# Sliding attention with alternating heads, value products one clip later, and the copy of the late transposed probabilities moved behind all exponentials

## The reference

```python
def _sliding_window_attn(q, k, v):          # 32 clips, 8 heads, 125 positions, 16 features
    for o in range(-32, 33):
        s = einsum('bhsd,bhsd->bhs', q, roll(k, -o)) * scale
        s = where((pos + o >= 0) & (pos + o < S), s, -inf)
    ...
    p = softmax(scores, axis=-1)
    ...
    out = out + p[..., idx:idx+1] * roll(v, -o)
...
qkv  = layernorm(h) @ W_qkv + b_qkv
h    = h + attention(q, k, v) @ W_proj + b_proj
out  = h + layernorm(h)                      # the last stage, whose other columns lie beyond the 128 there are
```

## Time and profile before

| what | value |
|---|---|
| median of 3 runs | 547.76 us (547.48 to 548.02) |
| profiled run | 550.68 us |
| span of the profiled run | 548.9 us, mean granted clock 0.947 |
| busy: PE, PEld, DVE, ACT, POOL | 503.3, 355.3, 408.9, 358.4, 329.2 us |
| exponentials of the windows (L972) | first starts at 390.8, last at 535.3 us |

### The profile page before, as it was taken

How to read it: one execution, slowest core, us unless ns; L and a number is a source line. 1 busy time by engine, 2 the same in 40 slices (tenths; PEclk the granted TensorE clock), 3 DMA queues, 4 the chain that set the end, 5 groups by cost and what they waited for, 6 DMA issues and landing times.

```text
span 548.9 us, 13987 instructions
## 1 busy us (share of the span) xinstructions
PE 503.3 (92%) x4554; PEld 355.3 (65%) x4554; DVE 408.9 (74%) x1728; ACT 358.4 (65%) x1072; POOL 329.2 (60%) x367
## 2 busy tenths in 40 slices
PE   6998899999998599999999999997599999999983
PEld 4778666666665357766667776655367766776762
DVE  3797757888886367787877777865369988898993
ACT  5985558889887244454455445453578888888881
POOL 2860647778886556776666676663126555565654
PEclk9999559999999699999999999999779999999997
DMA  4440212222222010000000000000000000000000
GB/s 163 138 161 11 64 34 51 56 62 62 63 60 75 20 37 20 19 20 22 35 22 20 19 20 20 1 1 1 0 2 2 20 21 20 13 11 21 20 21 20
DMA packets 21946, 19.89 MB, mean 36 GB/s; under 512 B 14210, under 2 KB 18466, under 8 KB 21746
## 3 DMA queue, kind: packets, MB, share of 16 engines
q1 hardware_dynamic: 21298, 18.28, 11.6%
q10 hardware_dynamic: 576, 0.71, 0.4%
HBM read 16.81 MB, written 2.18 MB: 35 GB/s over the span
## 4 chain that ended last, share of the span: by engine, by line
PE 44%; DVE 15%; issue 4%; ACT 2%; POOL 2%; POOLq 0%; DVEq 0%; ACTq 0%
PE quad L802 10%; PE quad L779 9%; PE bank L824 6%; PE bank L888 4%; PE bank L899 4%; DVE quad L1156 4%; PE bank L905 3%; PE quad L771 2%; PE bank L880 2%; DVE z_all L1186 2%; DVE otok L1168 2%; DVE st_all L1188 2%; DVE wmax L1156 2%; PE bank L793 1%; PE bank L817 1%
## 5 line engine op out<-in xcount | busy, mean ns | idle before, releaser
L476 POOL TENSOR_SCALAR put<-keyb,c 100x1000 f32<-100x1000 bf16 x32 | 89.0, 2782 | 47.9 <-DMA keyb<-key_scratch 26.3
L972 ACT ACTIVATE wprobs<-quad,wmax 125x125 f32<-125x125 f32 x256 | 75.5, 372 | 19.7 <-DVE wmax L1156 19.7
L1156 DVE CUSTOM_DVE_ANT_0 quad<-quad,c 125x125 f32<-125x125 f32 x256 | 66.1, 311 | 9.1 <-PE quad L847 9.1
L609 ACT ACTIVATE probs<-quad,negmax 100x250 f32<-100x250 f32 x128 | 58.3, 467 | 21.8 <-DVE negmax L561 20.9
L779 PE MATMUL quad<-h1T,w 128*128 128x500 f32 x128 | 61.9, 609 | 0.7 <-ACT hid L943 0.6
L802 PE MATMUL quad<-w,hid 128*125 128x128 f32 x512 | 58.8, 273 | 0.1
L802 PEld LDWEIGHTS quad<-w,hid 128*125 128x125 f32 x512 | 57.3, 188 | 0.8 <-issue 0.5
L1058 POOL TENSOR_TENSOR kbd<-wkT,c 128x250 f32<-128x250 f32 x32 | 19.2, 600 | 53.0 <-ACT wkT L980 53.0
L491 PE MATMUL bank<-c,probs 100*125 100x100 f32 x256 | 48.3, 316 | 2.2 <-ACT probs L609 1.4
L491 PEld LDWEIGHTS bank<-c,probs 100*125 100x125 f32 x256 | 36.8, 209 | 20.6 <-issue 13.2
L943 ACT ACTIVATE hid<-quad,vec_cols 128x500 f32<-128x500 f32 x64 | 43.0, 675 | 7.4 <-PE quad L779 4.1
(11 more groups left out here) (131 smaller groups left out, 1267.9 us busy)
## 6 DMA issues: line engine op xcount, KB each, us to landing
keyb<-key_scratch SPq DMA_DIRECT2D x64, 97.7 KB
xa<-xT SPq DMA_DIRECT2D x8, 500.0 KB, 3.6
xt<-xtok SPq DMA_DIRECT2D x16, 250.0 KB
out<-o_all SPq DMA_DIRECT2D x7, 250.0 KB
w<-weights SPq DMA_DIRECT2D x1, 1024.0 KB, 7.2
vec_rows<-rows SPq DMA_DIRECT2D x1, 448.0 KB, 5.2
c<-consts ACTq DMA_DIRECT2D x1, 428.5 KB, 6.5
w<-weights ACTq DMA_DIRECT2D x1, 192.0 KB, 4.2
```

Of the source, the lines that this page charges most:

```text
L476: nc.gpsimd.tensor_scalar(put[u % 3][:, :, :], keyb[p][:, :, :], c[0:ROWS, CONST["sidx"]], None, ALU.is_equal).then_inc(put_done, 1)
L609: nc.scalar.activation(probs[p][:, ch, :], s_bank[ch][0:ROWS, 0:L], ACT.Exp, bias=negmax[p][:, ch:ch + 1], accum_out=rowsum[p][:, ch:ch + ...
L972: ins = nc.scalar.activation(probs[p][:, j, :], s_of(j), ACT.Exp, bias=negmax[p][:, j:j + 1], scale=-1.0)
L1156: ins = nc.vector.tensor_tensor_reduce(s_of(j), s_of(j), c[0:LH, CONST["band"]], 1.0, OFF, ALU.add, ALU.min, negmax[p][:, j:j + 1])
```

## The change

Heads are worked on in the order 0, 2, 4, 6, 1, 3, 5, 7 (`ORDER`), so that neighbours in time lie in different banks. The transposed probabilities and the products are stored in that order, and the scaling of `otok` puts the heads back. Each mask and each exponential signals by itself (the counts go by 8 in place of 4), and the mask of the fifth to eighth head waits for the exponential of the head four places before it. The value products work on clip u-2 in window u, and everything behind them is one window later too. There is a third buffer `vo`, `y_of` and the projection lie in other columns, and the drain is one window longer.

The order changes too. On TensorE the `y_a` transposes stand ahead of the late transposes, and the value products go between the key and query products and the value matmul, ahead of `y_of`:

```diff
+                if within(u, 3, B + 3):
+                    pe.wait_ge(oT_done, u - 2)
+                    for i in range(2):
+                        ins = nc.tensor.transpose(y_a[:, 128 * i:128 * i + 128], oT[:, LH * i:LH * i + LH], ident)
+                    ins.then_inc(otok_ready, 1)
...
+                if within(u, 2, B + 2):
+                    wait(pe, otok_done, u - 2)
+                    wait(pe, oT_done, u - 2)
+                    pe.wait_ge(pT0_done, u - 1)
+                    pe.wait_ge(pT1_done, u - 1)
+                    pe.wait_ge(v_done, u - 1)
...
+                    for j in range(H):
+                        ins = nc.tensor.matmul(y_bank[CW * (j % 4):CW * (j % 4) + CW, LH * (j // 4):LH * (j // 4) + LH],
+                                               vo[(u - 2) % 3][:, ORDER[j], :], probsT[p][:, j, :], start=True, stop=True)
+                    ins.then_inc(pv_ready, 1)
+
                 if within(u, -1, B - 1):
                     wait(pe, qT_done, min(u + 2, B))
                     wait(pe, v_done, u + 1)
                     nc.tensor.matmul(x_v, n3T_all[:, LH * (u + 1):LH * (u + 1) + LH], w[:, WEIGHT["wv"]], start=True, stop=True).then_inc(v_ready, 1)
 
-                if within(u, 2, B + 2):
-                    pe.wait_ge(otok_done, u - 1)
+                if within(u, 3, B + 3):
+                    pe.wait_ge(otok_done, u - 2)
                     nc.tensor.transpose(y_of, otok[:, :], ident[0:LH, 0:LH]).then_inc(oF_ready, 1)
```

On ACT `woT` moves from behind `vo` to behind `kT`, and the exponentials of all heads stand together ahead of the copy of the late transposed probabilities:

```diff
+                def exponents(lo, hi):
+
+                    for k in range(lo, hi):
+                        j = ORDER[k]
+                        act.wait_ge(min_done, H * u + k + 1)
+                        nc.scalar.activation(probs[p][:, j, :], s_of(j), ACT.Exp, bias=negmax[p][:, j:j + 1], scale=-1.0).then_inc(exp_done, 1)
...
                 if within(u, 0, B):
                     wait(act, pT0_ready, u - 1)
-                    exponents(0)
-                    exponents(1)
+                    exponents(0, 8)
                 if within(u, 1, B + 1):
                     act.wait_ge(pT1_ready, u)
                     wait(act, pv_ready, u - 2)
                     nc.scalar.activation(probsT[1 - p][:, 4:8, :].rearrange("p h l -> p (h l)"), t_bank[1][0:LH, 0:4 * LH], ACT.Copy).then_inc(pT1_done, 1)
-                if within(u, 0, B):
-                    exponents(2)
-                    exponents(3)
```

On DVE the masks come as 2, 4 and 2 with the reciprocal and `otok` behind the first two and `oF` behind the next four, and `z_all` goes ahead of the copy:

```diff
+                if within(u, 0, B):
+                    dve.wait_ge(scores, u + 1)
+                    mask_and_min(0, 2)
...
+                if within(u, 0, B):
+                    mask_and_min(2, 6)
+                if within(u, 3, B + 3):
+                    dve.wait_ge(oF_ready, b + 1)
+                    wait(dve, proj_ready, b)
                     nc.vector.tensor_scalar(oF[:, :], y_of, col("wv_b"), None, ALU.add).then_inc(oF_done, 1)
                 if within(u, 0, B):
-                    mask_and_max(3)
+                    mask_and_min(6, 8)
+                if within(u, 3, B + 3):
+                    dve.wait_ge(proj_ready, b + 1)
...
+                    nc.vector.tensor_tensor(z_all[:, b:b + 1, :], y_proj.unsqueeze(1), z_all[:, b:b + 1, :], ALU.add).then_inc(z_done, 1)
+                if within(u, 0, B):
                     dve.wait_ge(pT0_ready, u + 1)
                     wait(dve, pv_ready, u - 1)
                     nc.vector.tensor_copy(probsT[p][:, 0:4, :].rearrange("p h l -> p (h l)"), t_bank[0][0:LH, 0:4 * LH]).then_inc(pT0_done, 1)
```

More of the change, by code:

```diff
@@ L725, in ffn_and_window @@
         x_k, x_q, x_v = x_bank[:, 0:LH], x_bank[:, 128:128 + LH], x_bank[0:LH, 256:256 + D]
-        y_a, y_of, y_proj = y_bank[0:LH, 256:512], y_bank[:, 0:LH], y_bank[0:LH, 256:256 + D]
+        y_a, y_of, y_proj = y_bank[0:LH, 256:512], y_bank[:, 256:256 + LH], y_bank[0:LH, 384:384 + D]
+        ORDER = (0, 2, 4, 6, 1, 3, 5, 7)
         def s_of(head):
@@ L856, in window @@
                     for j in range(4):
-                        ins = nc.tensor.transpose(t_bank[1][0:LH, LH * j:LH * j + LH], probs[pm][:, 4 + j, :], ident[0:LH, 0:LH])
+                        ins = nc.tensor.transpose(t_bank[1][0:LH, LH * j:LH * j + LH], probs[pm][:, ORDER[4 + j], :], ident[0:LH, 0:LH])
                     ins.then_inc(pT1_ready, 1)
-                if within(u, 2, B + 2):
[L861 to L864, removed]
                 if within(u, -2, B - 2):
@@ L887, in window @@
                     for j in range(4):
-                        ins = nc.tensor.transpose(t_bank[0][0:LH, LH * j:LH * j + LH], probs[p][:, j, :], ident[0:LH, 0:LH])
+                        ins = nc.tensor.transpose(t_bank[0][0:LH, LH * j:LH * j + LH], probs[p][:, ORDER[j], :], ident[0:LH, 0:LH])
                     ins.then_inc(pT0_ready, 1)
[L891 to L904, removed]
+                if within(u, 3, B + 3):
+                    pe.wait_ge(oF_done, u - 2)
                     nc.tensor.matmul(y_proj, oF[:, :], w[:, WEIGHT["wp"]], start=True, stop=True).then_inc(proj_ready, 1)
             in_turn(pe, ffn, window)
-            for u in range(B, B + 2):
+            for u in range(B, B + 3):
                 at(window, u)
@@ L980, in window @@
                     nc.scalar.activation(kT[:, :], x_k, ACT.Identity, bias=col("wk_b")).then_inc(kT_done, 1)
+                if within(u, 3, B + 3):
+                    act.wait_ge(pv_ready, u - 2)
+                    wait(act, otok_ready, u - 3)
+                    wait(act, z_done, u - 3)
+                    nc.scalar.activation(oT[:, :], y_bank[:, 0:2 * LH], ACT.Copy).then_inc(oT_done, 1)
+                if within(u, -1, B - 1):
                     wait(act, scores, u)
@@ L984, in window @@
                     act.wait_ge(v_ready, u + 1)
[L985 to L991, removed]
+                    wait(act, pv_ready, u - 2)
+                    nc.scalar.activation(vo[u % 3][:, :, 0:HD], x_v.rearrange("p (h f) -> p h f", h=H), ACT.Copy).then_inc(v_done, 1)
                 if within(u, 0, B):
                     wait(act, pT0_ready, u - 1)
-                    exponents(0)
-                    exponents(1)
+                    exponents(0, 8)
                 if within(u, 1, B + 1):
@@ L1073, in _ @@
             in_turn(pool, ffn, window)
-            for u in range(B, B + 3):
+            for u in range(B, B + 4):
                 at(window, u)
@@ L1148, in window @@
                 u, _, _ = shift(h, p, 0)
[L1149 to L1157, removed]
-                if within(u, 0, B):
-                    mask_and_max(0)
-                    mask_and_max(1)
@@ new lines, in window @@
+                if within(u, 3, B + 3):
+                    dve.wait_ge(otok_ready, b + 1)
+                    nc.vector.reciprocal(rinv[:, :], y_a.rearrange("p (h f) -> p h f", h=H)[:, :, HD]).then_inc(rinv_done, 1)
+                    dve.wait_ge(rinv_done, b + 1)
+                    wait(dve, oF_ready, b)
+                    nc.vector.tensor_tensor(otok[:, :].rearrange("p (k c f) -> p c k f", k=4, c=2),
+                                            y_a.rearrange("p (c k f) -> p c k f", c=2, k=4)[:, :, :, 0:HD],
+                                            rinv[:, :].rearrange("p (c k) -> p c k", c=2).unsqueeze(3).to_broadcast([LH, 2, 4, HD]),
+                                            ALU.mult).then_inc(otok_done, 1)
```

69 lines of the change are left out of this document (30 added, 39 removed).

## The result

The changed kernel took 562.16 us (561.53 to 562.58, 4 runs) against 547.62 for the kernel before: 1.027 times as long, 95% interval 1.0247 to 1.0293. The forecast was 563.3.

What follows compares the result with a forecast made beforehand. TensorE's late `y_of` holds DVE's `oF` and the masks behind it: 1.41 + 2.22 + 0.32 + 0.89 = 4.84 us a window; 13.6 - 2.0 + 3.9 = +15.5 us on 547.76 gives 563.3 us, range 558.5 to 567 (73%).

Steps and rivals of the forecast that it cites:

- The chain: Last exponential, late copy, `kT`, `woT`, `y_a`, TensorE's work before `y_of`, `oF`, two masks, last exponential: window 4.84 us against 4.37.
- The cause: `y_of` comes late on TensorE, so DVE waits at `oF` with the last two heads' masks queued behind it.
- The idle time: DVE stands idle before `oF`, waiting for TensorE's `y_of`: 0.6 us a window.
- What the change saves does not reach the end of the window: First exponential starts 0.25 us sooner, but the last goes by the last mask; order and single signals costed at nothing.
- Number of windows and ends: 29 windows at +0.47 give +13.6 us, windows 1 and 2 save 2.0, the longer drain adds 3.9: +15.5 us.
- The circle through the projection: `oF`, projection, `z_all`, copy, statistics, next masks: not what is waited for, with 0.2 us to spare.
- Neighbours on DVE: Operations around `oF` overlap; under the skill page's drain rule they would not, some 0.2 us more, window 5.0 us.
- the clock: Expected to stay at 1.00 (2.4 GHz); rival that it falls to 1.2 GHz for good, +60 us, 2%.
- The rivals: `woT` not holding 8%, `oF` not waited for 5%, no change 3%, clock falls 2%, slower than forecast 9%.
- `oF` was waited for: Second rival denied this: `y_of` ends before DVE's sixth mask is done, window 4.0 us, time 539, 5%.
- The first rival: `woT` does not hold TensorE, `y_a` starts behind the scores: window 4.48 us, time 552.9, 8%.
- the hold: On TensorE `y_a` waits for `woT` until T + 1.41, though TensorE is free at T + 1.05.

Runs made afterwards that it cites:

- the run with `oF` late: Changed kernel with DVE's `oF` behind the last two heads' masks and the early transposes' copy ahead of `z_all` again: window 4.35 us, 551.0 us in all.
- the run with pairs: Changed kernel with heads in natural order and both exponentials of a bank waiting for both its masks: window 5.06 us, 571.16 us in all.
- the run with the copy in the middle: Changed kernel with the late copy back between the fourth and fifth exponential on ACT: window 4.53 us, 555.21 us in all.
- the kernel before with the copy last: Kernel before with only the late copy moved behind all exponentials, value products still of clip u-1 in window u: 624.04 us, ratio 1.1381.

## Why the prediction was right, point by point

**The chain.** It foretold four parts from one `exponential` start to the next: 1.41 to the start of `y_a`, 2.22 to `y_of`, 0.32 to `oF`, 0.89 to the last exponential. The rows after give 471.34 - 469.93 = 1.41, 2.19, 0.31 and 0.90. The sum was 4.84 and is 4.81. 469.93 is 474.74 less a window. The value products with the change of shape took 1.11 from 472.10 to 473.21 with keys and queries, foretold 1.14. Six runs each altered one link, and each moved the window by what the chain had made one expect of that link, to within 0.05 us, up (two) or down (four).

**The cause.** DVE's `oF` waits for `y_of`, with two masks behind it. In the run with `oF` late a window is 0.46 us shorter, all of the 0.44 that the change had added. The idle time was put at 0.6, and the profile has 0.44. That counts from the end of the sixth mask's read, 473.25 + 0.14 = 473.39. From the read's start, which is nearly where the prediction's sum has DVE ready, it is 0.59. The term enters no sum.

**What alternation is worth.** Here the prediction's words failed: "What the change saves does not reach the end of the window", with the single signals costed at nothing. Its own arithmetic had the saving in it, because it let the last exponential follow 0.04 us behind the last mask's read. With signals by pairs both exponentials of the bank wait for that mask, and the last starts 0.25 later, which is what the run with pairs gives back (5.06). Without that saving the sum would have come out at 5.1. A step that reads "costs nothing" should be checked for what the sum would be without it.

**Number of windows and ends.** Foretold 13.6 for 29 windows, -2.0 for the first two and +3.9 for the drain, 15.5 in all. By the rows it is 29 x 0.44 = 12.8 for the windows, 10.3 - 12.8 = -2.5 for the rest between first and last exponential, and +4.6 for the drain, together 14.9. The windows were put 0.8 too high and the drain 0.7 too low, and these two nearly cancelled. The -2.5 has two parts. From the first exponential of window 1 to that of window 3 it was 410.68 - 401.16 = 9.52 us and is 404.28 - 396.47 = 7.81, which is 1.7 of the 2.0 foretold. The prediction left out the other part: the last two windows before the drain are shorter than 4.81, with last exponentials at 532.47, 537.10 and 541.23, so 4.63 and 4.13.

**The circle through the projection** was put at 0.2 us to spare. The trace of the changed kernel bears it out. Before the change the reciprocal starts together with the read of the mask ahead of it, at 467.67; in the changed kernel that read starts at 471.65 and the reciprocal at 471.87, right behind the end of `y_a` at 471.34 + 0.48 = 471.82. So DVE had 0.22 us to spare there.

**Neighbours on DVE, and the clock.** `oF` starts at 473.84, takes 0.35, and the mask behind it starts at 474.10, before its end; the window is 4.81. The page "VectorE: DVE Perf Modes" of the Trainium skill, section "The DRAIN you can't avoid", says that the next operation does not start until the pipe is empty, and by that a window would have been 5.0 us, an estimate of the prediction. The same section also says that a next operation that is not held starts earlier, which the prediction didn't mention, and the trace agrees with this second sentence. The clock stayed at 1.00 from 450 to 500 us. The page "TensorE: Matmul & The Clock Gate" of the Trainium skill, section "Part 1: The HAM clock gate (the "warmup" mystery)", says that the throttled state is the default and activity releases it; nothing in this trace speaks against that. The prediction had TensorE's waits elsewhere: it named 0.36 us before `y_a` and about 0.4 before the projection, and the trace has 0.21 before `y_a`, none before the projection and 0.52 before the scores.

**The rivals.** None came. `woT` did hold TensorE (0.21 us in each window), the clock held, and `oF` was waited for. The first rival's window of 4.48, without `woT`'s hold, is close to what the run with the copy in the middle reached, 4.53. That puts the hold at 0.28 us, where the prediction had 1.41 - 1.05 = 0.36: its scores start 0.42 behind the last exponential's start, and they start at 470.43 - 469.93 = 0.50.

## What to carry to other kernels

When work is moved ahead on an in-order engine, list who waits for what now stands behind it, and what is queued behind that waiting instruction on its own engine; here 1.0 us of value products and value matmul went in front of a small transpose, and two masks that had nothing to do with it paid. Try the parts of such a change one by one: alternating banks, with a signal for each head, gained 1.2% alone, the clip's distance alone lost 2.4% and the copy behind the exponentials alone lost 14%. And a longer pipeline must be paid for at its end and in buffers: here 4.6 us of drain, and, with the value products in their old place, a third buffer without which a copy waits in every window.

## What the runs showed of the hardware that I had not expected

In the kernel before with the copy last, the clock fell to 0.50 and rose to 1.00 again and again, though TensorE's longest single wait from 430 to 530 us was 1.8 us; the waits for the copy were 1.4 to 1.6 us in windows at either level. So neither such a wait nor its length tells which level a window gets, and no run here shows what does. In the changed kernel, with waits of 0.52 and 0.21, the clock held at 1.00 from 450 to 500 us. A delay on TensorE's path can so cost more than its own length: a window was 5.95 us at 1.00 and 7.16 on average.

Doubling the eight value products cost 0.43 us, and the first eight had taken 0.56 to the next instruction. The other 0.13 us don't grow with the number of products. That they belong to the change of shape beside them is likely and not shown.
